# A fused two-layer kernel: small tables, the order of mixing, the weights' queue and a bias product in its first loop

## What is computed

```python
Q, K, V = (norm(x) @ wq, ctx @ wk, ctx @ wv)          # 16 heads of 8 channels, over 64 positions
corr = irfft(rfft(Q) * conj(rfft(K)))                   # per channel, along the sequence
top_vals, top_idx = top_k(corr, 4)
w = softmax(top_vals)
out = sum(w[i] * roll(V, top_idx[i] mod 8 channels))    # channels of a head rotated
x = x + out @ wo
...
h = bitlinear(norm(x), w1, b1)                          # rows quantised to 8 bits, weights to -1, 0, 1
x = x + bitlinear(gelu(h), w2, b2)
```

## Time and profile before

| | |
|---|---|
| median of 3 runs | 1721.38 us (1720.53 to 1723.71) |
| the profiled execution | 1717.49 us, its span 1715.7 us, mean granted clock 0.947 |
| busy in the span | TensorE 1451.0, VectorE 1437.1, ScalarE 1256.9, GpSimd 1093.6 us |
| first loop | from 34 us (first load of x) to 429 us |
| DMA | 97.20 MB, mean 57 GB/s |

### The profile page before, as it was taken

One profiled execution on the slowest core, in us unless ns is written; L12 is line 12 of the kernel. 1 busy time (PEld: TensorE's weight loads), 2 busy tenths in 40 slices (PEclk: granted clock), 3 DMA queues, 4 the chain that ended last, 5 costly groups with the idle time before them and its releaser, 6 DMA issues. The chain is left out here.

```text
span 1715.7 us, 52980 instructions
## 1 busy us (share of the span) xinstructions
PE 1451.0 (85%) x17213; PEld 1224.8 (71%) x17213; DVE 1437.1 (84%) x4166; ACT 1256.9 (73%) x3770; POOL 1093.6 (64%) x1433
## 2 busy tenths in 40 slices
PE   4888889985699999999999999999999937999960
PEld 3766677763588887787778778777877825888850
DVE  3588899996799999999999999899989835888868
ACT  1367677874699988898898888888988815666640
POOL 1466666663566577777777777777777664666650
PEclk7999999998799999999999999999999967999995
DMA  4553443400000000000000000000000002332219
GB/s 136 173 194 132 159 149 137 148 1 1 15 7 7 7 13 14 18 16 12 12 15 15 11 12 17 11 12 15 15 11 8 13 30 80 83 86 79 76 34 294
DMA packets 101783, 97.20 MB, mean 57 GB/s; under 512 B 13256, under 2 KB 87275, under 8 KB 101504
## 3 DMA queue, kind: packets, MB, share of 16 engines
q1 hardware_dynamic: 79168, 70.02, 12.8%
q0 software_dynamic: 8640, 16.87, 3.0%
q10 hardware_dynamic: 13824, 8.39, 1.7%
HBM read 39.32 MB, written 56.83 MB: 56 GB/s over the span
## 5 line engine op out<-in xcount | busy, mean ns | idle before, releaser
L958 POOL TENSOR_TENSOR c_p<-c_p,c_rden 128x512 f32<-128x512 f32 x256 | 266.4, 1041 | 175.6 <-DVE c_rden L1023 173.6
L1163 ACT ACTIVATE c_p<-bank,c_nmax 128x128 f32<-128x128 f32 x1024 | 362.8, 377 | 3.8 <-DVE c_nmax L1009 3.8
L1163 ACT ACTIVATION_READ_ACCUMULATOR c_p<-bank,c_nmax 128x1 f32 x1024 | 223.0, 218 | 0.0
L1334 POOL DMA_INDIRECT moe_outputs<-e_y,e_rows x142 | 153.4, 1080 | 93.4 <-DVE e_y L1363 56.4
L1009 DVE TENSOR_REDUCE c_nmax<-bank 128x4 f32<-128x512 f32 x256 | 174.4, 681 | 39.8 <-PE bank L104 36.0
L102 PE MATMUL bank<-c_kvT,qk_fused 128*128 128x128 f16 x1024 | 188.9, 222 | 1.8 <-ACT c_kvT L1142 1.4
L103 PE MATMUL bank<-c_kvT,qk_fused 128*128 128x128 f16 x1024 | 188.8, 222 | 0.0
L104 PE MATMUL bank<-c_kvT,qk_fused 128*128 128x128 f16 x1024 | 188.8, 222 | 0.0
L1230 PE MATMUL bank<-const,c_p 128*128 128x128 f32 x1024 | 156.4, 275 | 13.3 <-DVE c_pT0rest L1034 12.6
L1402 ACT ACTIVATE e_h<-bank,moe_b 128x256 f32<-128x256 f32 x284 | 118.2, 466 | 65.6 <-PE bank L104 64.2
L998 POOL DMA_INDIRECT moe_slots<-r_rows,r_pos x128 | 131.0, 1023 | 35.9 <-issue 35.9
(11 more groups left out here) (296 smaller groups left out, 6062.6 us busy)
## 6 DMA issues: line engine op xcount, KB each, us to landing
moe_slots<-slot_fill SPq DMA_DIRECT2D x66, 516.0 KB, 5.3
e_rows<-moe_slots SPq DMA_DIRECT2D x71, 129.0 KB, 2.4
f_z<-moe_outputs SPq DMA_DIRECT2D x32, 256.0 KB, 4.8
x<-in_x SPq DMA_DIRECT2D x16, 256.0 KB, 3.1
a_ctx<-in_ctx SPq DMA_DIRECT2D x32, 128.0 KB, 3.2
moe_stage<-in_L_ffn_W ACTq DMA_DIRECT2D x16, 256.0 KB, 3.1
c_ctx<-in_ctx SPq DMA_DIRECT2D x128, 32.0 KB, 2.0
out_x<-x ACTq DMA_DIRECT2D x16, 256.0 KB, 4.7
```

Source lines behind the costliest of these rows:

```text
L958: pool.tensor_tensor(pr[r % 4][:], pr[r % 4][:], rep(rden[r % 4][:], 2, P), ALU.mult).then_inc(m["pn"], 1)
L1163: last = act.activation(pr[r % 4][:, h, :], SB[r % 2][:, P * h:P * h + P], ACT.Exp, bias=nmax[r % 4][:, h:h + 1], accum_out=den[r % 4][:, ...
L1334: pool.indirect_dma_start(s.z, bass.IndirectOffsetOnAxis(ap=xr[t % XBUF][:, h, 2 * D:ROW].bitcast(U32), axis=0), ys[t % YBUF][:, h, :], No ...
```

## The change

1. `choose`: the constant table `iota_e` holds (channel - e) mod 8 instead of e, so the roll table is only index AND 7 (one operation less, L473 gone), and the comparison is with that table.
2. The DMAs of expert weights go from ScalarE's queue to SyncE's, between the loads of a group and the fill DMAs; SyncE waits for `w_split`.
3. The bias: `diagonal` is replaced by `inverse_parts` on GpSimd: the inverse scale as three bf16 parts, each three times, in 9 of 32 columns per tile. It stands after `norm`, before `split_weights`. TensorE transposes them (once a step, behind the row transposes, which now wait for `parts`) into the same bank, ScalarE copies 640 instead of 512 columns, and the bias product is a bf16 product with `bit_b1_rows`, the three bf16 parts of b1 laid out in matching rows, which VectorE makes once, in step 1 (`bias_rows`).
4. TensorE: the mixing of values goes ahead of `turn_hidden` 0 and `correlate`; expansion 3 goes ahead of `turn_hidden` 0; `values` and `project_out` go ahead of a `contract` each. ScalarE follows: Gelu 3 behind Gelu 2, and the copy of mixed ahead of the hidden copies.
5. ScalarE: a one-column Gelu before the copy of kk and a one-column Exp behind Gelu 3, into an unused tile `table`, which put the table loads there.

```diff
-    out[:, C_IE:C_IE + 32] = np.repeat(np.arange(8), TOP)[None]
+    out[:, C_IE:C_IE + 32] = (ch[:, None] - np.repeat(np.arange(8), TOP)[None]) % 8
+    for part in range(3):
+        out[:, C_PART + part] = (ch % 32 < 9) & (ch % 32 % 3 == part)
+    for j in range(4):
+        out[:, C_TILE + j] = ch // 32 == j
...
+                if 2 <= g < EXPERTS + 2:
+                    e = g - 2
+                    if e:
+                        sp.wait_ge(w_split, e)
+                    sp.dma_start(stage[:, 0, :], dram["L1_ffn_W1"][e, :, :]).then_inc(w_in, 16)
...
-                wait(pool, mb["h"], 4 * g)
-                pool.tensor_tensor(diag[:], rep(s.ident, 1, GT), rep(inv[:], 2, P), ALU.mult).then_inc(mb["diagonal"], 1)
+                wait(pool, mb["qt"], g)
+                pool.tensor_tensor(ip[:, :, 0:3], rep(inv[:], 2, 3), three, ALU.mult)
+                pool.drain()
+                pool.tensor_tensor(ir[:, 0, :], inv[:], ip[:, :, 0], ALU.subtract)
+                pool.drain()
+                pool.tensor_tensor(ip[:, :, 3:6], rep(ir[:, 0, :], 2, 3), three, ALU.mult)
+                pool.drain()
+                pool.tensor_tensor(ir[:, 1, :], ir[:, 0, :], ip[:, :, 3], ALU.subtract)
+                pool.drain()
+                pool.tensor_tensor(ip[:, :, 6:9], rep(ir[:, 1, :], 2, 3), three, ALU.mult).then_inc(mb["parts"], 1)
...
+                if a := at(i, k, -2):
+                    inverse_parts(a[0])
                 if known(i) and 0 < 2 * i + k <= EXPERTS:
                     split_weights(i, k, 2 * i + k - 1)
                 if a := at(i, k, -3):
                     hidden_scale(a[0], a[1])
-                if a := at(i, k, -2):
-                    diagonal(a[0])
...
-                dve.tensor_scalar(roll[:], ix[:, :, 0:TOP], -1.0, s.chan, ALU.mult, ALU.add)
-                dve.drain()
-                dve.tensor_scalar(roll[:], roll[:], 7, None, ALU.bitwise_and)
+                dve.tensor_scalar(roll[:], ix[:, :, 0:TOP], 7, None, ALU.bitwise_and)
...
+            def bias_rows():
+                hi, mid, lo, all_ = (q2[0][:, n, :] for n in range(4))
+                rest = ge[0][:, 0, :]
+                dve.tensor_copy(hi, s.bit_b1[:])
+                dve.drain()
+                dve.tensor_tensor(rest, s.bit_b1[:], hi, ALU.subtract)
...
+                for j in range(GT):
+                    last = dve.tensor_scalar(s.bit_b1_rows[:, j, :], all_, s.tile_rows[:, j:j + 1], None, ALU.mult)
...
                 if a := at(i, k, 0):
                     choose(a[0])
+                if known(i) and 2 * i + k == 1:
+                    bias_rows()
...
+                if b:
+                    act.activation(table[:], s.eps[:, 0:1], ACT.Gelu)
                 if new:
                     copy_kk(g, 0)
...
                     gelu(b[0], b[1], 2)
+                    gelu(b[0], b[1], 3)
+                if new:
+                    act.drain()
+                    act.activation(table[:], s.eps[:, 0:1], ACT.Exp)
+                if b:
                     square(b[0], b[1], 2)
...
-                if known(i) and 2 * i + k < EXPERTS:
-                    load_weights_of(2 * i + k)
...
+                pe.wait_ge(mb["parts"], g + 1)
+                last = pe.transpose(QT[:, P * GT:P * GT + P], ip[:].rearrange("p j a -> p (j a)"), s.ident_b[:])
...
-                if j == 0:
-                    pe.wait_ge(mb["diagonal"], g + 1)
-                pe.matmul(HB[j % 2][:], diag[:, j, :], s.bit_b1[:], start=False, stop=True).then_inc(mb["h"], 1)
+                pe.matmul(HB[j % 2][:], qt[p][:, P * GT:P * GT + P], s.bit_b1_rows[:, j, :], start=False, stop=True).then_inc(mb["h"], 1)
...
-                if done:
-                    turn_hidden(i, k, done[0], done[1], 0)
+                if old:
+                    await_values(old[0])
                 if b:
                     expand(i, k, b[0], b[1], 3)
                 if old:
-                    await_values(old[0])
+                    mix_values(old[0])
+                if done:
+                    turn_hidden(i, k, done[0], done[1], 0)
                 if new:
                     correlate(new[0], k)
```

More of the change, by code:

```diff
@@ L268, in first_layer @@
                "rows rows_copied mixed mixed_copied out x1")
-    b_names = "mv r1 amax scale q qt qt_copied h inverse diagonal gelu sq amax2 scale2 q2 q2t q2t_copied product x2 xb2"
+    b_names = "mv r1 amax scale q qt qt_copied h inverse parts bias_rows gelu sq amax2 scale2 q2 q2t q2t_copied product x2 xb2"
     ma = {n: sem("a_" + n) for n in a_names.split()}
@@ L307, in first_layer @@
         qb = [sb(f"b_q{n}", [P, GT, D], BF16) for n in range(2)]
-        qt = [sb(f"b_qt{n}", [P, GT * P], BF16) for n in range(2)]
+        qt = [sb(f"b_qt{n}", [P, GT * P + P], BF16) for n in range(2)]
         inv = sb("b_inverse", [P, GT])
-        diag = sb("b_diagonal", [P, GT, P])
+        ip = sb("b_inverse_parts", [P, GT, 32], BF16)
+        ir = sb("b_inverse_rest", [P, 2, GT])
         ge = [sb(f"b_gelu{n}", [P, GT, FF]) for n in range(2)]
@@ L320, in first_layer @@
         q2t = [sb(f"b_q2t{n}", [P, 2, KB, P], BF16) for n in range(2)]
+        table = sb("a_table", [P, 1])
         stage = sb("moe_stage", [P, 2, FF])
@@ L533, in hidden @@
                     dve.tensor_reduce(am2[:, j:j + 1], ge[k][:, j, :], AX.X, ALU.max, apply_absolute_value=True).then_inc(mb["amax2"], 1)
+            def bias_rows():
[4 more added lines that the diff above has]
+                dve.tensor_tensor(rest, s.bit_b1[:], hi, ALU.subtract)
+                dve.drain()
+                dve.tensor_copy(mid, rest)
+                dve.drain()
+                dve.tensor_tensor(lo, rest, mid, ALU.subtract)
+                dve.tensor_scalar(all_, hi, s.part_rows[:, 0:1], None, ALU.mult)
+                dve.drain()
+                dve.scalar_tensor_tensor(all_, mid, s.part_rows[:, 1:2], all_, ALU.mult, ALU.add)
+                dve.drain()
+                dve.scalar_tensor_tensor(all_, lo, s.part_rows[:, 2:3], all_, ALU.mult, ALU.add)
+                dve.drain()
+                for j in range(GT):
+                    last = dve.tensor_scalar(s.bit_b1_rows[:, j, :], all_, s.tile_rows[:, j:j + 1], None, ALU.mult)
+                last.then_inc(mb["bias_rows"], 1)
             def invert(g, k):
@@ L662, in step @@
                     gelu(b[0], b[1], 2)
+                    gelu(b[0], b[1], 3)
[3 more added lines that the diff above has]
+                if b:
                     square(b[0], b[1], 2)
+                if old:
+                    act.wait_ge(ma["mixed"], old[0] + 1)
+                    wait(act, ma["out"], old[0])
+                    act.activation(mixed[:].rearrange("p b r -> p (b r)"), MIX[:], ACT.Copy).then_inc(ma["mixed_copied"], 1)
                 if done:
                     copy_hidden(done[0], 0)
-                if b:
-                    gelu(b[0], b[1], 3)
                 if new:
@@ L677, in step @@
                     high_weights(2 * i + k - 1)
-                if old:
-                    act.wait_ge(ma["mixed"], old[0] + 1)
-                    wait(act, ma["out"], old[0])
-                    act.activation(mixed[:].rearrange("p b r -> p (b r)"), MIX[:], ACT.Copy).then_inc(ma["mixed_copied"], 1)
                 if new:
@@ L700, in turn_rows @@
                 for j in range(GT):
-                    last = pe.transpose(QT[:, P * j:P * j + P], qb[p][:, j, :], s.ident_b[:])
+                    pe.transpose(QT[:, P * j:P * j + P], qb[p][:, j, :], s.ident_b[:])
+                pe.wait_ge(mb["parts"], g + 1)
+                last = pe.transpose(QT[:, P * GT:P * GT + P], ip[:].rearrange("p j a -> p (j a)"), s.ident_b[:])
                 last.then_inc(mb["qt"], 1)
@@ L780, in expand @@
                 pe.matmul(HB[j % 2][:], qt[p][:, P * j:P * j + P], s.bit_w1[:], start=True, stop=False)
-                if j == 0:
-                    pe.wait_ge(mb["diagonal"], g + 1)
-                pe.matmul(HB[j % 2][:], diag[:, j, :], s.bit_b1[:], start=False, stop=True).then_inc(mb["h"], 1)
+                if known(g) and 4 * g + j == 0:
+                    pe.wait_ge(mb["bias_rows"], 1)
+                pe.matmul(HB[j % 2][:], qt[p][:, P * GT:P * GT + P], s.bit_b1_rows[:, j, :], start=False, stop=True).then_inc(mb["h"], 1)
             def turn_hidden(i, k, g, p, r):
```

28 lines of the change are left out of this document (14 added, 14 removed).

## The result

The changed kernel takes 1703.46 us (median of four runs, 1701.37 to 1706.43), the kernel before on the same chip 1720.95 (1717.58 to 1723.71): a ratio of 0.9906 with an interval of 0.9889 to 0.9922. It is faster by 17.5 us where 24.0 were forecast. The profiled execution took 1701.37, its span 1699.5, its mean granted clock 0.944. In the loop the gain is 11.5 us, less than half of the forecast.

A forecast was written before the change was run, and what follows sets the result against it. VectorE's own instructions bound step 10; in steps 4 to 10 it also waited for ScalarE's copy. Savings of 16.4 (steps 4 to 10), 2.3 (10 to 15), 1.3 (ramp) and 4.0 (tail): 1721.4 - 24.0 = 1697.4 us, range 1687 to 1711.

The forecast's parts named there:

- the first rival: ScalarE's chain still ends last, with slack of only 0.2 to 0.4 us: 0.6 us in 12 steps, 1706 us; chance 0.20.
- the first steps' term: Steps 0 to 4: waits 5.2, L473 2.0, L489 0.8, less bias_rows 5.5 and mixing 1.15; gain 1.3 us.
- Steps 4 to 9, 16.4 forecast: Steps 4 to 10, product to product: gain of 8.8 + 3.7 + 3.9 = 16.4 us.
- the 8.8 forecast: Steps 4 to 10: five VectorE waits for ScalarE's copy L613 go, with weights on SyncE and table loads moved; 8.8 us.
- The 3.9 for L489: Steps 4 to 10: VectorE's scaling L489 loses its stall as GpSimd's diagonal goes; 5 x 0.77 = 3.9 us.
- The 3.7 for L473: Steps 4 to 10: int32 operation L473 goes; 3.7 us, taken between 1.9 and 5.5.
- the end that I had worked out from it: Pessimistic end for removing L473, steps 4 to 10: stalls are passed on, 6 x 0.32 = 1.9 us.
- Steps 10 to 14 and the tail: Steps 10 to 15: gain 1.6 + 0.7 = 2.3 us; tail, steps 16 to 19: gain 4.0 us.
- Feed-forward rows behind mixing: Mixing ahead of correlation: 0 from step 4, 1.15 us cost in step 1; earlier Gelu 3 hidden by VectorE's queue.
- The clock: Rival: TensorE, idler, drops to a lower clock each step, 2.6 us in 13 steps; slower than before, 1731 us; chance 0.07.
- The last rival: Gain hidden: GpSimd bounds steps 4 to 9 or x loads queue behind fills; most of 16.4 lost, 1719 us; chance 0.05.
- the 405 that I had named as a sign: Sign that the forecast is right: the loop ends at 405 us instead of 429.

The follow-up runs named there:

- e10: The kernel before with only the expert weights' DMAs moved to SyncE's queue; one run, 1701.68 us, loop 366.72 us.
- e3: The changed kernel without the one-column Gelu and Exp, so the tables load where Exp and Gelu stand; ratio to before 0.9928, loop 366.35 us.
- e6: The changed kernel with the roll table by channel minus index again (L473 back, with its drain); ratio to before 0.9893, loop 373.11 us.
- e7: The changed kernel with the old order of TensorE and ScalarE (correlation ahead of mixing, expansion 3 behind first q2 transposes); one run, 1709.49 us.
- e11: The changed kernel with bias_rows in step 0 and GpSimd's addition of b2 behind inverse_parts; ratio to before 1.0018, loop 374.90 us.
- e1: The changed kernel with bias_rows in step 0, ahead of the first product, instead of step 1; ratio to before 0.9858, loop 355.80 us.
- e2: The changed kernel with correlation and its copy ahead of mixing until the feed-forward part has begun; ratio to before 0.9897, loop 361.54 us.
- e5: The changed kernel with GpSimd's diagonal and the float32 bias product again, without bias_rows; ratio to before 0.9936, loop 369.79 us.
- c0: The changed kernel run again without an edit, as control; ratio to before 0.9908, loop 367.86 us.
- e9: The changed kernel with both bias_rows in step 0 and the early correlation ahead of mixing; ratio to before 0.9835, loop 357.41 us.
- e4: The changed kernel with the expert weights' DMAs back on ScalarE's queue at its step's end; ratio to before 0.9982, loop 372.96 us.

## Why the prediction was right and where it was wrong

**The whole.** 1703.5 us lies in the stated range, and its gain of 17.5 us is nearer to the forecast's 24.0 than the loop's 11.5. That is luck in part: up to some 4 us of it arise outside the loop and aren't the change's (below). The time is also nearer to the first rival's 1706 than to 1697.4, but the rival's mechanism isn't what happened: ScalarE's chain isn't late in the steady steps. The step of the prediction that failed is the first steps' term.

**Steps 4 to 9, 16.4 forecast, 15.1 measured.** The waits for kk went (0 at each of steps 5 to 10 after the change), and undoing queue and one-column loads costs 9.1, near the 8.8 forecast. Two things about them were not in the prediction. I took the waits as ScalarE's time alone. Of the 8.8 us of before some 3.3 were TensorE's clock: the waits of the five steps were 1.19, 2.85, 1.21, 2.87 and 0.66, TensorE idled 2.50 to 2.60 us ahead of each of the first four, and only the two long ones stand behind stretches like these, with 1.00 at the others:

```profile
159.40:164.00 4.60, 4.51 (x21) 4.15 (x22) 2.85 (x11) 1.40 (x4) 3.64 (x3) 0.63 0.00 0
207.12:211.50 4.38, 4.38 (x20) 4.02 (x21) 2.75 (x10) 1.31 (x3) 3.53 (x3) 0.61 0.00 0
```

I had row 207.12 at hand and read it as what might come, while it was what was there and would go. And the queue alone, on the kernel before, gives 8.6 (e10), so the one-column loads matter only with the other parts, which make VectorE's step shorter: 2.5 then (e3), in one step. The 3.9 for L489 came whole (all at 0.22 to 0.23 in these steps). The 3.7 for L473 did not: e6 gives 2.0. These prices don't add: undone one by one (e3 to e7) they come to 19.8 us in steps 4 to 9, where the whole change brought 15.1.

**The stall that was passed on.** In steps 4 to 8 ev takes 0.81 to 1.10 where the earlier trace rows had 0.17, because it is now the next small instruction while GpSimd's split runs:

```profile
178.33 0.81 DVE L494 TENSOR_TENSOR a_ev<-a_top 128x32 f32<-128x32 f32 x1
179.24 0.18 DVE L497 TENSOR_SCALAR a_roll<-a_idx 128x32 uint32<-128x32 uint32 x1
```
```profile
176.83 2.27 POOL L445 TENSOR_TENSOR moe_weight_parts<-moe_stage,moe_weight_parts 128x512 f16<-128x512 f32 x2
```

It ends at 179.14, with the split at 179.10. By the Trainium skill (SBUF — State Buffer, SBUF: two separate sides) the shared pair is an exclusive lock held for a whole instruction. This row, e6 and e11 agree with that: a stall lasts until a GpSimd instruction ends, and isn't removed with the instruction that met it. So I should have taken the end that I had worked out from it, 1.9 instead of 3.7. Steps 4 to 8, with the split, are 20.5 to 21.0 long, steps 9 to 13 20.1 to 20.6.

**Steps 0 to 3, 1.3 of gain forecast, 8.0 of loss measured.** This is the term that failed, and it is three things. bias_rows was sized at 5.5, and its instructions take 5.5, but in its place it costs 10.7 (e1): I added its length to the path and did not ask what idles meanwhile. TensorE does, 4.92 us, and its clock falls to 0.70 over step 2. Nor did I follow the chain through the new order, in which mixing stands ahead of the correlation; 1.15 was its time on a free TensorE at full clock, where here it carries GpSimd's lateness with it. That is 5.2. Another 1.6 is step 0 at 14.60 instead of 12.97, which can't be put down to a part of the change: e10, with the queue alone, has 14.60, and e2 and e3, which undo another part each, have 12.97. The last 2.5 is what the other parts brought less than the 6.85 that I had for them: e1, without the price of bias_rows, gains 4.4 there. Which of them fell short isn't shown. (The upper end of 6.5 that I gave for bias_rows doesn't follow either: its terms add up to 6.8.)

**Steps 10 to 14 and the tail.** 1.35 and 3.0 measured, 2.3 and 4.0 forecast. In the tail the expansion waits 0.80 us for qt instead of 3.17 for the diagonal, and the last scale comes 58.9 us behind the product of step 15, before 61.9. e5 and e10, with the diagonal, both have 71.48: it is the parts that shorten the tail.

```profile
393.23 0.39 PE L824 MATMUL bank<-bit_w,b_qt 128*128 128x512 bf16 x1 [0.80 <-ACT b_qt L675]
```

**Feed-forward rows behind mixing, forecast 0 from step 4.** Nothing was added, so the term stands, but I took from it that the order doesn't matter. Undone it costs 8.8 us from step 4 to 15 (e7, one execution), of which the first steps give 5.3 back. Its worth is that it shortens TensorE's gap ahead of q2, which my sum had no line for. I wrote that the gain of Gelu 3 is hidden by VectorE's queue, and in the step of e7 that is shown it is: what comes late is the correlation.

**The rivals.** ScalarE's chain: at none of steps 5 to 10 does the product wait, though the slack that I called 0.2 to 0.4 us is as thin as said: in e11, e3 and e6 waits of 0.7 to 2.7 us appear, the longer of them with a fallen clock. The clock: after the change it is 1.00 from 122 to 347 us although TensorE is busy 103.54 of 123.47 us only (17.3 us a step, where I had 16.1). There the rival falls, and with it, for this stretch, what the Trainium skill (TensorE: Matmul & The Clock Gate, HAM oscillation) made me weigh; e11 and e7 show that it was one edit away. The idle time of steps 4 to 14 lies mostly in three places, 0.41 to 0.71 us ahead of the transpose of the parts, 0.97 to 1.73 ahead of spectrum 2 and 1.00 to 1.47 ahead of q2's transposes, and no piece is long. The last rival's time doesn't follow from its terms: with all of the 16.4 lost, 1697.4 gives 1713.8, not 1719. It wasn't met: GpSimd's parts make TensorE wait 0.4 to 0.7 us from step 4 on, without effect on the product. The loop ended at 415 us, not at the 405 that I had named as a sign.

**The account.** The loop explains 11.5 of the 16.2 us between the two profiled spans; 2.6 lie ahead of it and 2.1 behind it. Neither is the change's: with the same preparation the first product came at 47.29 in one execution of the changed kernel and at 49.90 in another, and the part behind the loop took 1284.5 to 1290.3 us in the six traces of before, after, c0, e7, e10 and e11. But the interval of the ratio gives 13.4 to 19.1 us for the whole. With step 0 alike in both, the loop would give 13.1. What makes up the rest, up to some 4 us, stays open.

**A version with a shorter loop than both** is e1, or e9, which can't be told from it: 0.9858 [0.9804, 0.9913] and 0.9835 [0.9776, 0.9893] to before. So both beat the kernel before, but these intervals reach into that of the change (0.9908 [0.9893, 0.9923] in c0), which e1 beats by its loop alone: 11.9 us, or 10.3 with step 0 alike. In the loop e1 is 23.4 us below before, nearly the 24.0 that was forecast for the change.

## What to carry to other kernels

Price a one-time operation by what idles behind it, not by its length: 5.5 us in front of four engines cost 10.7, and in a wait that was there anyway 0. When a wait of a steady stretch alternates between two lengths, look at the granted clock in both steps before taking it for the named engine's: filling TensorE's gap ahead of q2 was worth 8.8 us from step 4 on here (e7), more than taking L473 away. Try each part of a change alone and undone; one of five alone brought as much as the whole in the loop, and its undoing in the whole showed only 6.6 of the 8.6. And before naming what an instruction waits for, hold the releaser shown against the waits in the source: the row maximum that seemed to wait for Gelu 3 waits for another copy.

## What the runs showed of the hardware that was not expected

- The clock after an idle piece is not settled by its length: after 2.61 and 2.62 us it was 0.65 and 1.00 (e4), after 2.27 and 2.25 us 0.62 and 1.00 (e3), after 2.06 it was 0.65 (e6), after 2.9 it mostly alternated (e11), and after the 1.7 of five steps of the kernel after it was 1.00, though 0.62 after 1.95 in its step 2. Step 0 took 12.97 or 14.60 us in kernels whose instructions there are the same, with a clock of 1.00 or 0.88, after the same 2.12 or 2.13 us of idling, which alone moves a comparison of single executions by 1.6 us. Both traces of the changed kernel have 14.60, so whether it belongs to a kernel or to an execution stays open.
- Some of VectorE's small instructions were stretched beside GpSimd's (ev of 128x32, L535 of 128x4, the int32 operation, L489 of 128x64), by 0.5 to 0.9 us. In e11, where L535 no longer stood beside one, the four operations of 128x128 behind it took 2.51 instead of 0.88 us.
- All that follows the loop, which the change doesn't touch, took 1284.5 to 1290.3 us in six traces, and 1348.3 to 1362.2 in the eight on the two slower chips.
